# A fused residual kernel whose attention stage receives its row maxima through SyncE instead of GpSimd, with the first two bodies' score products made twice

## The chip, the cores and the metric

The kernel runs on one core of one Trainium2 chip. Its time is the device time of one execution, in microseconds (us). The engines are TensorE (PE in the profile, PEld for its weight loads), VectorE (DVE), ScalarE (ACT), GpSimd (POOL) and SyncE (SP, which here only issues DMAs). The kernel before takes 488.98 us, the median of 3 runs (486.17 to 490.18).

## What is computed

The input `x` is [16, 128, 128]: 16 batches of 128 positions with 128 features. Four residual steps follow each other:

```
x = x + L0(x)   # reflected second differences along both axes and a growth term, per-batch factors
x = x + L1(x)   # 8 gated experts and a shared one: (silu(x @ Wg) * (x @ Wu)) @ Wd, weighted per batch
x = x + L2(x)   # low-rank product with the batch's language, and the language's embedding
x = x + L3(x)   # attention, 16 heads of 8 features
```

The attention is the step that matters here:

```
query = seq2 + b_self
key = jnp.concatenate([seq1 + b_prev, seq2 + b_self], 1)
...
score_prev = jnp.einsum('bhqd,bhkd->bhqk', q, k[:, :, :l1]) * SCALE
score_self = (q * k[:, :, l1:]).sum(-1, keepdims=True) * SCALE
mask = jnp.arange(l1)[None, :] < seq_len1[:, None]
...
weights = jax.nn.softmax(jnp.concatenate([score_prev, score_self], -1), axis=-1)
attn = jnp.einsum('bhqk,bhkd->bhqd', weights[..., :-1], v[:, :, :l1])
attn = attn + weights[..., -1:] * v[:, :, l1:]
```

Each query attends to the 128 masked positions of one sequence and to one score of its own; the softmax subtracts each row's maximum over both.

## The kernel before, in words

**Stages.** The 16 batches are taken as four tiles of 4 (TB). The first 379 us are the experts: for each tile, 36 slots (`SLOTS`) of gate, up and down products, each product as three matmuls of rounded parts (`three`, L516 to L518). The last 110 us are the attention, one `body` for each batch b from 0 to 15; bodies 2 to 13 run in a loop of four bodies. The low-rank step and the keys and values of the last tile (`LAST_AUX`: lora_a, lora_b, key, value, x_natural) are spread over bodies 0 and 1.

**Data of a batch.** Queries and keys are kept in HBM as rows (`q_rows`, `k_rows`). SP loads them for a pair p of batches (2p and 2p + 1): `load_first(p)` fills `k_blocks` and `q_plain` (4 DMAs of 96 KB, one of 16 KB, one of 384 KB), `load_second(p)` fills `q_blocks` and `k_plain` (4 of 96 KB, one of 384 KB). There are two buffers of each.

**Two score products.** `scores(b, i)` (into `s_ps`, L585) gives scores with the queries on the partitions; VectorE reduces each to row maxima (`max_group`, L1151) and merges them (`merge_max`, L1159). It is made two bodies ahead: body b makes the scores of b + 2. GpSimd negates and splits the maxima (`split_max`, L1361 to L1366), TensorE turns them (`turn_max`, L592), ScalarE copies them out as `max_rows` (`copy_max`, L868), and two DMAs of 8 KB (`place_max`, L1351) put them as two more rows into `q_blocks`. `scores_t(b, i)` (into `st_ps`, L684) then gives the transposed scores with the maximum already subtracted, ScalarE takes the exponential (`exp_scores`, L915), and `weigh` (L694) multiplies with the values. `scores_t(b, 0)` is the instruction that waits for the two DMAs (`max_placed`). After that come `take_pv` (ACT), `turn_pv` (PE, L703), `normalise` (DVE, L1214 to L1220), `turn_attn` (PE, L709), `copy_attn` (ACT, L935) and `project` (PE, L713), each one or two batches late.

**What sets the order.** Every engine runs its own written list in order, with semaphore waits. In body b TensorE turns the maxima of b + 2 at the end. GpSimd in body b does `split_max(b + 2)`, `weigh_self(b)`, `place_max(b + 2)`. So `max_rows` go through GpSimd's own DMA queue (q0 in the profile), while SP's DMAs are on q1. SP's list after the first four loads is `step(p)` for each pair: `load_first(p + 2)` once the scores of batches up to 2p + 1 are written, `load_second(p + 1)` once the transposed scores up to 2p - 1 are written, then `store_out(p - 3)`. Ahead of `step(2)` stand `later_stores(NT - 1)`: six DMAs of 128 KB that put the last tile's key rows into HBM. The last tile's steps and `turn_max` use one and the same PSUM bank (`aux_ps` and `max_ps` are the same eighth of PSUM), `out_ps` is the bank that the experts' `acc_ps` leaves.

## Time and profile before

| | |
|---|---|
| median of 3 runs | 488.98 us (486.17 to 490.18) |
| profiled execution | 490.55 us; its span, first to last instruction, 488.7 us |
| busy over the span | PE 441.0 us, DVE 341.5, ACT 273.2, POOL 210.9 |
| mean granted TensorE clock | 0.952 of full speed |
| DMA | 30.68 MB, of which q1 (SP and ACT) 29.99 MB, q0 (GpSimd) 0.26 MB |

Times of rows are us from the start of the span. A row of the timeline has start, duration, engine, line, operation with output and inputs, shape and count; in square brackets stands how long the engine was idle before it and what ended that. A matmul's duration is longer than its share of the engine, since matmuls overlap: the engine's share is the distance between starts. "issue" after an arrow says that the profile names no releaser. The start of a batch in the attention is read here as the start of its first `scores_t`, the first L684 row of a body.

### The profile page before, as it was taken

How to read it: one execution, taken by the hardware profiler on the slowest of the kernel's cores; microseconds unless marked ns; L12 is line 12 of the kernel's file. 1: busy time of each engine (PE TensorE's matmuls, PEld its weight loads, DVE VectorE, ACT ScalarE, POOL GpSimd, SP SyncE). 2: the span in 40 equal slices, each digit the busy share in tenths (PEclk: the TensorE clock that was granted, in tenths of full speed). 3: DMA queues.
4: the chain of work that ended last, by engine and by line, in shares of the span. 5: the costliest groups of instructions: out<-in, count | busy, mean ns of one | idle time of the engine just before them, and what ended most of it. 6: DMA issues, size and time to landing. Idle time of an engine off the chain costs nothing.

```text
span 488.7 us, 7752 instructions
## 1 busy us (share of the span) xinstructions
PE 441.0 (90%) x2278; PEld 330.3 (68%) x2278; DVE 341.5 (70%) x594; ACT 273.2 (56%) x544; POOL 210.9 (43%) x261
## 2 busy tenths in 40 slices
PE   5789699779999998999999999999999778888894
PEld 2668578567678787867878686787787354545552
DVE  5787567597777779677768967776796666565552
ACT  2647556546465555545565554556556546565573
POOL 4667666883223434222244323228557333243340
PEclk9889979989999999999999999999999898797798
DMA  5423322300002020000201000022025256555320
GB/s 155 128 72 108 124 66 83 110 23 22 2 0 87 1 67 0 21 0 0 83 3 53 11 0 1 0 65 67 0 67 145 56 158 171 134 128 139 78 58 23
DMA packets 28147, 30.68 MB, mean 63 GB/s; under 512 B 4084, under 2 KB 22616, under 8 KB 28120
## 3 DMA queue, kind: packets, MB, share of 16 engines
q1 hardware_dynamic: 26664, 29.99, 21.8%
q0 software_dynamic: 1024, 0.26, 0.3%
q8 instruction: 13, 0.21, 0.2%
q10 hardware_dynamic: 432, 0.10, 0.1%
q14 instruction: 14, 0.11, 0.1%
HBM read 22.73 MB, written 7.35 MB: 62 GB/s over the span
## 4 chain that ended last, share of the span: by engine, by line
PE 63%; DVE 13%; DMA 8%; ACT 6%; issue 5%; POOL 4%; DVEq 0%; ACTq 0%; SPq 0%; POOLq 0%
PE acc_ps L516 6%; PE g_ps L516 5%; PE acc_ps L518 5%; PE g_ps L518 5%; PE acc_ps L517 5%; PE g_ps L517 5%; DVE act_lo L1086 5%; PE u_ps L516 5%; PE u_ps L518 4%; PE u_ps L517 4%; DMA w_raw<-in_L_cond_Wu 4%; DVE act_p L1082 3%; DMA q_blocks<-max_rows 3%; PE pv_ps L694 2%; PE s_ps L585 2%
## 5 line engine op out<-in xcount | busy, mean ns | idle before, releaser
L815 ACT ACTIVATE act_p<-g_ps 128x512 f32<-128x512 f32 x144 | 86.0, 597 | 135.2 <-PE g_ps L518 120.5
L1082 DVE TENSOR_TENSOR act_p<-act_p,u_ps 128x512 f32<-128x512 f32 x144 | 98.6, 685 | 71.5 <-PE u_ps L518 44.5
L1086 DVE TENSOR_TENSOR act_lo<-act_p,act_hi 128x512 fp32r<-128x512 f32 x144 | 121.1, 841 | 0.2 <-ACT act_hi L820 0.2
L1296 POOL TENSOR_TENSOR xg_lo<-xg,xg_hi 128x512 fp32r<-128x512 f32 x35 | 50.5, 1442 | 147.1 <-ACT xg_hi L825 147.1
L820 ACT ACTIVATE act_hi<-act_p 128x512 fp32r<-128x512 f32 x144 | 89.8, 624 | 3.8 <-DVE act_p L1082 3.5
L516 PE MATMUL acc_ps<-act_hi,w_split 128*128 128x512 f32 x144 | 62.0, 430 | 16.8 <-DVE act_lo L1086 16.7
L516 PE MATMUL g_ps<-x_hi,w_split 128*128 128x512 f32 (+1 forms) x144 | 57.8, 402 | 1.4 <-DVE x_lo L1112 1.4
L518 PE MATMUL acc_ps<-act_hi,w_split 128*128 128x512 f32 x144 | 57.2, 397 | 0.0
L516 PE MATMUL u_ps<-xg_hi,w_split 128*128 128x512 f32 x144 | 57.0, 396 | 0.1
L518 PE MATMUL g_ps<-x_hi,w_split 128*128 128x512 f32 (+1 forms) x144 | 56.9, 395 | 0.0
L517 PE MATMUL g_ps<-x_lo,w_split 128*128 128x512 f32 (+1 forms) x144 | 56.9, 395 | 0.0
L517 PE MATMUL acc_ps<-act_lo,w_split 128*128 128x512 f32 x144 | 56.9, 395 | 0.0
L517 PE MATMUL u_ps<-xg_lo,w_split 128*128 128x512 f32 x144 | 56.5, 392 | 0.0
L518 PE MATMUL u_ps<-xg_hi,w_split 128*128 128x512 f32 x144 | 56.4, 392 | 0.0
L1285 POOL TENSOR_TENSOR w_split<-w_raw,w_split 128x512 fp32r<-128x512 f32 x27 | 40.1, 1487 | 27.2 <-ACT w_split L786 27.2
L516 PEld LDWEIGHTS acc_ps<-act_hi,w_split 128*128 128x128 f32 x144 | 27.3, 189 | 34.5 <-DVE act_lo L1086 24.0
L1151 DVE TENSOR_REDUCE max_key<-s_ps 128x4 f32<-128x512 f32 x56 | 36.4, 685 | 14.2 <-PE s_ps L585 13.4
L1292 POOL TENSOR_TENSOR xg<-x,gates 128x512 f32 (+1 forms) x35 | 40.9, 1169 | 5.8 <-ACT x L795 3.6
L684 PE MATMUL st_ps<-q_blocks,k_plain 98*128 98x512 f32 x64 | 31.1, 490 | 8.9 <-DMA q_blocks<-max_rows 5.8
L516 PEld LDWEIGHTS g_ps<-x_hi,w_split 128*128 128x128 f32 x144 | 27.5, 191 | 7.3 <-DVE x_lo L1112 1.7
L516 PEld LDWEIGHTS u_ps<-xg_hi,w_split 128*128 128x128 f32 x144 | 27.5, 191 | 6.6 <-issue 0.5
L518 PEld LDWEIGHTS g_ps<-x_hi,w_split 128*128 128x128 f32 x144 | 27.5, 191 | 6.1
(161 smaller groups left out, 718.2 us busy)
## 6 DMA issues: line engine op xcount, KB each, us to landing
k_blocks<-k_rows SPq DMA_DIRECT2D x32, 96.0 KB
q_plain<-q_rows SPq DMA_DIRECT2D x8, 384.0 KB
q_blocks<-q_rows SPq DMA_DIRECT2D x32, 96.0 KB
k_plain<-k_rows SPq DMA_DIRECT2D x8, 384.0 KB
w_raw<-in_L_cond_Wg SPq DMA_DIRECT2D x8, 256.0 KB, 2.7
w_raw<-in_L_cond_Wu SPq DMA_DIRECT2D x8, 256.0 KB, 2.9
w_raw<-in_L_cond_Wd SPq DMA_DIRECT2D x8, 256.0 KB, 2.8
q_rows<-rows_hi SPq DMA_DIRECT2D x16, 128.0 KB
```

The lines of the kernel that those rows point to most:

```text
L516: mm(dst, w_h, x_h, start=start, stop=False)
L517: mm(dst, w_h, x_l, start=False, stop=False)
L518: return mm(dst, w_l, x_h, start=False, stop=stop)
L684: mm(st_ps[i % 2][:], k_plain[n // 2 % 2][0:ROWS + 2, i, half(n)], q_blocks[n // 2 % 2][0:ROWS + 2, :, i, half(n)], start=True, stop=True) ...
L815: activation(act_p[k % 3][:], g_ps[k % 3][:], ACT.Silu).then_inc(silu_done, 1)
L820: activation(act_hi[k % 3][:], act_p[k % 3][:], ACT.Identity).then_inc(act_hi_done, 1)
L1082: tt(act_p[k % 3][:], act_p[k % 3][:], u_ps[k % 3][:], ALU.mult).then_inc(prod_done, 1)
L1086: tt(act_lo[k % 3][:], act_p[k % 3][:], act_hi[k % 3][:].bitcast(F32), ALU.subtract).then_inc(act_lo_done, 1)
L1151: nc.vector.tensor_reduce(max_key[n % 2][:, i], (s_ps[i % 2] if bank is None else bank)[:].rearrange("p (j s) -> p j s", j=GJ), AX_X, ALU. ...
L1285: tt(w_lo[:, w // 3, w % 3], w_raw[w % 3][:], w_hi[:, w // 3, w % 3].bitcast(F32), ALU.subtract)\
L1292: tt(xg[:], x1[:, t], over_s(gates[:, e, bass.ds(t * TB, TB)]), ALU.mult).then_inc(xg_made, 1)
L1296: tt(xg_lo[e % 3][:], xg[:].rearrange("p b s -> p (b s)"), xg_hi[e % 3][:].bitcast(F32), ALU.subtract)\
```

## The change

Four things are moved or rewritten, and one is added.

1. SP issues the two DMAs of `max_rows`. Its list becomes: `step(0)`; then for each batch b a wait for `max_copied` and `place_max(b)`; after each odd b from 3 on `step(b // 2)`; after batch 3 also the last tile's six row stores.
2. `turn_max(b + 1)` stands in body b behind the first score product, where `turn_max(b + 2)` stood at the end of it; ScalarE's `copy_max` and `exp_self` move likewise. `turn_attn(b - 2)` and its copy move forward to the middle of the body, `project` to before the last `scores_t`.
3. The last tile's steps use `out_ps`, so the waits for `max_copied` ahead of them and for `aux_drained` ahead of `turn_max` go; one wait is put ahead of the first `turn_attn`.
4. The own weight and the weighted own value lie in one buffer `own_w`, so that `normalise` has three instructions where it had four; GpSimd does `weigh_self(b)` first.
5. In bodies 0 and 1 every score product, of both kinds, is issued twice with the same operands and output (`FIRST_RUNS`).

```diff
+FIRST_RUNS = 2
+LAST_STORES = 3
...
-        self_exp = [sb2(f"self_exp{n}", [128, H]) for n in range(4)]
+        own_w = [sb2(f"own_w{n}", [128, H, DH + 1]) for n in range(4)]
...
+        def later_ps(t):
+
+            return out_ps if isinstance(t, int) and t == NT - 1 else aux_ps
...
+            def place_max(b):
+
+                for c in range(2):
+                    sp.dma_start(q_blocks[b // 2 % 2][ROWS + c:ROWS + c + 1, :, :, b % 2 * S:(b % 2 + 1) * S]
+                                 .rearrange("p j i s -> p (j i) s").bitcast(F32),
+                                 max_rows[b % 2][c * H:(c + 1) * H]).then_inc(max_placed[b % 2], 16)
+
...
-            for p in range(NP + 3):
-                if p == 2:
+            step(0)
+            for b in range(B):
+                sp.wait_ge(max_copied, b + 1)
+                place_max(b)
+                if b % 2 and b > 1:
+                    p = b // 2
+                    if p == NP - 4:
+                        sp.wait_ge(rows_stored, ROW_STORES * 2 * NT)
+                    step(p)
+                if b == LAST_STORES:
                     later_stores(NT - 1)
-                if p == NP - 4:
-                    sp.wait_ge(rows_stored, ROW_STORES * 2 * NT)
+            for p in range(NP, NP + 3):
                 step(p)
             sp.wait_ge(out_stored, 16 * NP)
...
-                kind = LATER_AUX[m]
+                kind, ps = LATER_AUX[m], later_ps(t)
-                    last = mm(aux_ps[0:64, :], lora_a_t[:], x1[:, t].rearrange("p b s -> p (b s)"), start=True, stop=True)
+                    last = mm(ps[0:64, :], lora_a_t[:], x1[:, t].rearrange("p b s -> p (b s)"), start=True, stop=True)
...
-                mm((s_ps[i % 2] if bank is None else bank)[:], q_plain[n // 2 % 2][0:ROWS + 1, i, half(n)],
-                   k_blocks[n // 2 % 2][0:ROWS + 1, :, i, half(n)], start=True, stop=True).then_inc(s_written, 1)
+                for _ in range(FIRST_RUNS if isinstance(b, int) and bank is None else 1):
+                    last = mm((s_ps[i % 2] if bank is None else bank)[:], q_plain[n // 2 % 2][0:ROWS + 1, i, half(n)],
+                              k_blocks[n // 2 % 2][0:ROWS + 1, :, i, half(n)], start=True, stop=True)
+                last.then_inc(s_written, 1)
...
-                mm(st_ps[i % 2][:], k_plain[n // 2 % 2][0:ROWS + 2, i, half(n)],
-                   q_blocks[n // 2 % 2][0:ROWS + 2, :, i, half(n)], start=True, stop=True).then_inc(st_written, 1)
+                for _ in range(FIRST_RUNS if isinstance(b, int) and b < 2 else 1):
+                    last = mm(st_ps[i % 2][:], k_plain[n // 2 % 2][0:ROWS + 2, i, half(n)],
+                              q_blocks[n // 2 % 2][0:ROWS + 2, :, i, half(n)], start=True, stop=True)
+                last.then_inc(st_written, 1)
...
             def last_tile_step(b, i):
                 if isinstance(b, int) and (b, i) in LAST_AUX:
-                    pe.wait_ge(max_copied, b + 2)
                     later_step(LAST_AUX[b, i], NT - 1)
-            def body(b, n, s_next=True):
-
-                for i in range(2):
-                    if s_next:
-                        scores(b + 2, n + 2, i)
-                    scores_t(b, n, i)
+            def body(b, n, s_next=True, turn_next=True):
+
+                if s_next:
+                    scores(b + 2, n + 2, 0)
+                if n >= 1 and turn_next:
+                    turn_max(b + 1, n + 1)
+                scores_t(b, n, 0)
+                if s_next:
+                    scores(b + 2, n + 2, 1)
+                scores_t(b, n, 1)
                 last_tile_step(b, 1)
                 if n >= 1:
                     weigh(b - 1, n - 1, 0)
                     weigh(b - 1, n - 1, 1)
+                if n == 2:
+                    pe.wait_ge(aux_drained, LAST_STEP + 4)
+                if n >= 2:
+                    turn_attn(b - 2, n - 2)
                 if s_next:
                     scores(b + 2, n + 2, 2)
                     scores(b + 2, n + 2, 3)
                     weigh(b - 1, n - 1, 2)
                     weigh(b - 1, n - 1, 3)
                 if n >= 2:
-                    turn_attn(b - 2, n - 2)
+                    project(b - 2, n - 2)
                 scores_t(b, n, 3)
                 last_tile_step(b, 3)
-                if n >= 2:
-                    project(b - 2, n - 2)
                 if n >= 1:
                     turn_pv(b - 1, n - 1)
-                if isinstance(b, int) and b < 2:
-                    pe.wait_ge(aux_drained, LAST_STEP + (1 if b == 0 else 4))
-                if s_next:
-                    turn_max(b + 2, n + 2)
...
-                body(b, b % TB, s_next=False)
+                body(b, b % TB, s_next=False, turn_next=b + 1 < B)
...
-                activation(self_exp[n % 4][:], self_arg[n % 2][:], ACT.Exp).then_inc(self_exp_done, 1)
+                activation(own_w[n % 4][:, :, DH], self_arg[n % 2][:], ACT.Exp).then_inc(self_exp_done, 1)
...
-            def body(b, n, s_next=True):
+            def body(b, n, turn_next=True):
                 exp_scores(b, n, 0)
+                if n >= 1 and turn_next:
+                    copy_max(b + 1, n + 1)
+                    exp_self(b + 1, n + 1)
                 exp_scores(b, n, 1)
                 last_tile_step(b, 1)
                 if n == 0:
                     act.wait_ge(v_ones_set, 2)
                 place_values(b, n)
+                if n >= 2:
+                    copy_attn(b - 2, n - 2)
                 exp_scores(b, n, 2)
                 last_tile_step(b, 2)
                 if n >= 1:
                     take_pv(b - 1, n - 1)
-                if n >= 2:
-                    copy_attn(b - 2, n - 2)
                 exp_scores(b, n, 3)
-                if s_next:
-                    copy_max(b + 2, n + 2)
-                    exp_self(b + 2, n + 2)
...
-                dve.wait_ge(self_exp_done, b + 1)
-                tt(denom[n % 2][:], pv[:, :, DH], self_exp[n % 4][:], ALU.add).then_inc(norm_step, 1)
                 dve.wait_ge(self_weighted, b + 1)
-                tt(numer[n % 2][:], pv[:, :, 0:DH], v_self_w[n % 2][:], ALU.add).then_inc(norm_step, 1)
-                dve.wait_ge(norm_step, b * 3 + 2)
-                nc.vector.reciprocal(rdenom[n % 2][:], denom[n % 2][:]).then_inc(norm_step, 1)
-                dve.wait_ge(norm_step, b * 3 + 3)
-                tt(attn[n % 2][:], numer[n % 2][:], rdenom[n % 2][:].unsqueeze(2).to_broadcast([128, H, DH]),
+                tt(numer[n % 2][:], pv[:, :, 0:DH + 1], own_w[n % 4][:], ALU.add).then_inc(norm_step, 1)
+                dve.wait_ge(norm_step, b * 2 + 1)
+                nc.vector.reciprocal(rdenom[n % 2][:], numer[n % 2][:, :, DH]).then_inc(norm_step, 1)
+                dve.wait_ge(norm_step, b * 2 + 2)
+                tt(attn[n % 2][:], numer[n % 2][:, :, 0:DH], rdenom[n % 2][:].unsqueeze(2).to_broadcast([128, H, DH]),
                    ALU.mult).then_inc(attn_done, 1)
...
-            def weigh_self(b, n, place_next):
+            def weigh_self(b, n):
                 wait(pool, attn_done, b - 1)
                 pool.wait_ge(self_exp_done, b + 1)
-                if place_next:
-                    pool.wait_ge(max_copied, b + 3)
                 own = own_values[:].rearrange("p t (b x) -> p (t b) x", b=TB)[:, b].rearrange("p (h r) -> p h r", r=DH)
-                tt(v_self_w[n % 2][:], own, self_exp[n % 4][:].unsqueeze(2).to_broadcast([128, H, DH]),
-                   ALU.mult).then_inc(self_weighted, 1)
+                w = own_w[n % 4]
+                tt(w[:, :, 0:DH], own, w[:, :, DH:DH + 1].to_broadcast([128, H, DH]), ALU.mult).then_inc(self_weighted, 1)
             def body(b, n, s_next=True):
+                weigh_self(b, n)
                 if s_next:
                     split_max(b + 2, n + 2)
-                weigh_self(b, n, s_next)
-                if s_next:
-                    place_max(b + 2, n + 2)
                     pick_mask(b + 2, n + 2)
             for b in range(2):
-                pool.wait_ge(max_copied, b + 1)
-                place_max(b, b)
                 pick_mask(b, b)
```

SP's list in the attention, from the third pair's first loads on; `max_rows` are the maxima, `rows_hi` and `rows_lo` the last tile's keys. Before:

```order
L453 DMA k_blocks<-k_rows 24x1024 x4
L464 DMA k_blocks<-mask_row 1x16x256
L457 DMA q_plain<-q_rows 96x1024
L453 DMA k_blocks<-k_rows 24x1024 x4
L464 DMA k_blocks<-mask_row 1x16x256
L457 DMA q_plain<-q_rows 96x1024
L453 DMA q_blocks<-q_rows 24x1024 x4
L457 DMA k_plain<-k_rows 96x1024
L390 DMA k_rows<-rows_hi 4x32x256 x4
L390 DMA k_rows<-rows_lo 4x32x256 x2
L453 DMA k_blocks<-k_rows 24x1024 x4
```

And now:

```order
L457 DMA k_blocks<-k_rows 24x1024 x4
L468 DMA k_blocks<-mask_row 1x16x256
L461 DMA q_plain<-q_rows 96x1024
L487 DMA q_blocks<-max_rows 1x16x128 x8
L457 DMA k_blocks<-k_rows 24x1024 x4
L468 DMA k_blocks<-mask_row 1x16x256
L461 DMA q_plain<-q_rows 96x1024
L457 DMA q_blocks<-q_rows 24x1024 x4
L461 DMA k_plain<-k_rows 96x1024
L394 DMA k_rows<-rows_hi 4x32x256 x4
L394 DMA k_rows<-rows_lo 4x32x256 x2
L487 DMA q_blocks<-max_rows 1x16x128 x4
```

The eight rows of maxima DMAs are batches 0 to 3; those of batches 4 and 5 stand behind the 11 loads and the 6 stores. From there on four such DMAs (an even and an odd batch) stand between one pair's loads and the next.

TensorE's list at the start of the attention, bodies 0 and 1. Before, with `lora_a_t` and `lora_b_t` the last tile's low-rank step and L592 the turning of the maxima:

```order
L585 MATMUL s_ps<-k_blocks,q_plain 128x512
L684 MATMUL st_ps<-q_blocks,k_plain 128x512
L585 MATMUL s_ps<-k_blocks,q_plain 128x512
L684 MATMUL st_ps<-q_blocks,k_plain 128x512
L562 MATMUL aux_ps<-x,lora_a_t 64x512
L585 MATMUL s_ps<-k_blocks,q_plain 128x512 x2
L684 MATMUL st_ps<-q_blocks,k_plain 128x512
L564 MATMUL aux_ps<-dif_a,lora_b_t 128x512
L684 MATMUL st_ps<-q_blocks,k_plain 128x512
L592 MATMUL max_ps<-squares,neg_max 32x128
L585 MATMUL s_ps<-k_blocks,q_plain 128x512
L684 MATMUL st_ps<-q_blocks,k_plain 128x512
```

And now:

```order
L604 MATMUL s_ps0<-k_blocks1,q_plain1 128x512 x2
L705 MATMUL st_ps0<-q_blocks0,k_plain0 128x512 x2
L604 MATMUL s_ps1<-k_blocks1,q_plain1 128x512 x2
L705 MATMUL st_ps1<-q_blocks0,k_plain0 128x512 x2
L580 MATMUL out_ps<-x1,lora_a_t 64x512
L604 MATMUL s_ps0<-k_blocks1,q_plain1 128x512 x2
L604 MATMUL s_ps1<-k_blocks1,q_plain1 128x512 x2
L705 MATMUL st_ps0<-q_blocks0,k_plain0 128x512 x2
L582 MATMUL out_ps<-dif_a,lora_b_t 128x512
L705 MATMUL st_ps1<-q_blocks0,k_plain0 128x512 x2
L604 MATMUL s_ps0<-k_blocks1,q_plain1 128x512 x2
L612 MATMUL max_ps<-squares,neg_max0 32x128
```

Four more products stand ahead of the first low-rank product, and the first turning (L612, batch 2) comes behind the first score product of body 1 instead of ahead of it.

## Rows read from the trace of the kernel before

**Rows 1.** Timeline of TensorE: the first `scores_t` of batches 3 to 14, in order.

```profile
402.43 0.50 PE L684 MATMUL st_ps<-q_blocks,k_plain 98*128 98x512 f32 x1 [1.66 <-DMA q_blocks<-max_rows]
...
408.22 0.40 PE L684 MATMUL st_ps<-q_blocks,k_plain 98*128 98x512 f32 x1
...
416.55 0.47 PE L684 MATMUL st_ps<-q_blocks,k_plain 98*128 98x512 f32 x1 [2.98 <-issue]
...
423.08 0.63 PE L684 MATMUL st_ps<-q_blocks,k_plain 98*128 98x512 f32 x1
...
429.58 0.49 PE L684 MATMUL st_ps<-q_blocks,k_plain 98*128 98x512 f32 x1 [0.76 <-DMA q_blocks<-max_rows]
...
434.44 0.46 PE L684 MATMUL st_ps<-q_blocks,k_plain 98*128 98x512 f32 x1
...
441.19 0.47 PE L684 MATMUL st_ps<-q_blocks,k_plain 98*128 98x512 f32 x1 [1.75 <-DMA q_blocks<-max_rows]
...
448.28 0.57 PE L684 MATMUL st_ps<-q_blocks,k_plain 98*128 98x512 f32 x1
...
455.09 0.50 PE L684 MATMUL st_ps<-q_blocks,k_plain 98*128 98x512 f32 x1 [1.60 <-DMA q_blocks<-max_rows]
...
462.40 0.39 PE L684 MATMUL st_ps<-q_blocks,k_plain 98*128 98x512 f32 x1
...
472.27 0.70 PE L684 MATMUL st_ps<-q_blocks,k_plain 98*128 98x512 f32 x2
```

**Rows 2.** Timeline of SP: the first loads of each pair, and the last tile's stores.

```profile
391.22 1.52 SPq L453 DMA_DIRECT2D k_blocks<-k_rows  x4
...
395.98 3.26 SPq L390 DMA_DIRECT2D k_rows<-rows_hi  x4
399.29 2.84 SPq L390 DMA_DIRECT2D k_rows<-rows_lo  x2
404.82 1.92 SPq L453 DMA_DIRECT2D k_blocks<-k_rows  x4
...
419.23 1.52 SPq L453 DMA_DIRECT2D k_blocks<-k_rows  x4
...
431.85 1.53 SPq L453 DMA_DIRECT2D k_blocks<-k_rows  x4
...
444.45 1.91 SPq L453 DMA_DIRECT2D k_blocks<-k_rows  x4
```

**Rows 3.** Timeline of GpSimd: maxima of batches 3 and 5; then the tile's landing times.

```profile
396.18 1.03 POOL L1351 DMA_DIRECT2D q_blocks<-max_rows  x2
...
409.18 1.03 POOL L1351 DMA_DIRECT2D q_blocks<-max_rows  x2
...
DMA to landing us min/median/max: 1.7/2.7/6.7
```

**Rows 4.** Windows: length, busy PE, PEld, DVE, ACT, POOL, granted clock, DMA share, GB/s.

```profile
386.50:395.00 8.50, 7.93 (x62) 5.67 (x63) 4.86 (x10) 4.48 (x10) 2.44 (x9) 0.80 0.18 57
...
403.00:404.00 1.00, 1.00 (x19) 0.49 (x18) 0.69 (x1) 1.00 (x2) 0.12 (x1) 1.00 0.27 97
...
405.30:405.60 0.30, 0.30 (x12) 0.27 (x12) 0.30 (x1) 0.30 (x1) 0.00 (x0) 0.50 0.26 89
...
418.00:419.00 1.00, 1.00 (x6) 0.81 (x3) 0.19 (x1) 0.61 (x3) 0.00 (x0) 0.50 0.00 0
...
428.80:429.00 0.20, 0.02 (x1) 0.00 (x0) 0.17 (x2) 0.20 (x2) 0.00 (x0) 1.00 0.00 0
```

**Rows 5.** Timeline of TensorE, bodies 0 and 1: low-rank products and turnings.

```profile
382.22 1.10 PE L564 MATMUL aux_ps<-dif_a,lora_b_t 68*128 68x512 f32 x2 [0.41 <-DVE dif_a L1058]
...
386.46 0.27 PE L592 MATMUL max_ps<-squares,neg_max 128*32 128x128 f32 x1 [2.92 <-issue]
...
395.00 0.28 PE L592 MATMUL max_ps<-squares,neg_max 128*32 128x128 f32 x1 [0.57 <-DVE x L1070]
```

**Rows 6.** Timeline of ScalarE and TensorE, a body at full clock: the late copies.

```profile
437.98 0.27 ACT L935 ACTIVATE attn_t<-out_ps 128x128 f32<-128x128 f32 x1
...
438.31 0.49 PE L713 MATMUL out_ps<-w_raw,attn_t 128*128 128x128 f32 x2 [0.17 <-ACT attn_t L935]
```

More of the change, by code:

```diff
@@ L210, in build @@
         pv_own = [sb2(f"pv_own{n}", [128, HALVES, S]) for n in range(2)]
-        v_self_w = [sb2(f"v_self_w{n}", [128, H, DH]) for n in range(2)]
-        denom = [sb2(f"denom{n}", [128, H]) for n in range(2)]
         rdenom = [sb2(f"rdenom{n}", [128, H]) for n in range(2)]
-        numer = [sb2(f"numer{n}", [128, H, DH]) for n in range(2)]
+        numer = [sb2(f"numer{n}", [128, H, DH + 1]) for n in range(2)]
         attn = [sb2(f"attn{n}", [128, H, DH]) for n in range(2)]
@@ L570, in later_step @@
                         tok = slice(b * S, (b + 1) * S)
-                        last = three(aux_ps[:, tok], in_hi[:, tok], in_lo[:, tok], w_qkv_h[:, 2], w_qkv_l[:, 2])
+                        last = three(ps[:, tok], in_hi[:, tok], in_lo[:, tok], w_qkv_h[:, 2], w_qkv_l[:, 2])
                 else:
                     for b in range(TB):
-                        last = turn(aux_ps[:, b * S:(b + 1) * S], x3_t[:, b], ident)
+                        last = turn(ps[:, b * S:(b + 1) * S], x3_t[:, b], ident)
                 last.then_inc(aux_written, 1)
@@ L809, in later_step @@
                     act.wait_ge(rows_stored, (2 * NT - 1) * ROW_STORES if isinstance(t, int) and t == NT - 1 else t * (2 * ROW_STORES) + 2 * ROW_STORES)
-                    activation(rows_hi[:], aux_ps[:], ACT.Identity, bias=cols[:, 1:2]).then_inc(aux_rounded, 1)
+                    activation(rows_hi[:], later_ps(t)[:], ACT.Identity, bias=cols[:, 1:2]).then_inc(aux_rounded, 1)
             def silu(t, k):
@@ L966, in _ @@
             for b in range(B - 2, B):
-                body(b, b % TB, s_next=False)
+                body(b, b % TB, turn_next=b + 1 < B)
             take_pv(B - 1, B - 1)
@@ L1345, in _ @@
                         nc.gpsimd.memset(tile[:].bitcast(F32), constant).then_inc(blocks_filled, 1)
-            def place_max(b, n):
-                for c in range(2):
-                    pool.dma_start(q_blocks[n // 2 % 2][ROWS + c:ROWS + c + 1, :, :, n % 2 * S:(n % 2 + 1) * S]
-                                   .rearrange("p j i s -> p (j i) s").bitcast(F32),
-                                   max_rows[n % 2][c * H:(c + 1) * H]).then_inc(max_placed[n % 2], 16)
             def split_max(b, n):
```

16 lines of the change are left out of this document (8 added, 8 removed).

## The prediction

> **What bounds the kernel now.** I read the stretches first, then TensorE's order of work in the attention, then what it waits for. The experts (to 379 us) are untouched. The change lives in the last 110 us, and there I read where each batch starts [rows 1]. Batches 12 and 13 show what two bodies need when nothing holds them: 472.27 - 462.40 = 9.9 us, 4.9 us each. From batch 4 to batch 12 eight bodies take 462.40 - 408.22 = 54.2 us, 6.8 each. The 15 us between are two things. First, the odd batches 3, 5, 7, 9 and 11 wait 1.66, 2.98, 0.76, 1.75 and 1.60 us, 8.8 in all, in front of their first `scores_t` [rows 1]; the 2.98 has no releaser named, but the same instruction waits for the same DMAs. Second, behind each of these waits but the shortest TensorE's granted clock falls: in the window 418 to 419 us it is 0.50, 1.2 instead of 2.4 GHz [rows 4]. The body pairs behind such a wait show the price: 448.28 - 441.19 = 7.1 and 462.40 - 455.09 = 7.3 us for one body, so 2.3 us over 4.9 [rows 1]. After 0.76 us there is no such price (434.44 - 429.58 = 4.9).
>
> Why the odd ones? SP's loads of a pair start at 404.82, 419.23, 431.85 and 444.45 us [rows 2]; call such a moment L. The maxima of the odd batch are issued behind it (batch 5: 409.18 [rows 3]) and TensorE goes on at 416.55, 429.58, 441.19, 455.09 [rows 1], that is L + 11.7, 10.4, 9.3 and 10.6, on average **L + 10.5**. An 8 KB transfer in a free machine lands in 1.7 to 2.7 us [rows 3]; here it lands when the pair's 1.57 MB are through. In the window 428.80 to 429.00 nothing moves any more [rows 4], and TensorE resumes 0.8 us after 428.8. So it is the loads, and not GpSimd's two issues of 1.03 us together [rows 3], that make these waits.
>
> **The change part by part.** Times below are of the profiled execution (490.55 us, span 488.7), which lies 1.57 above the median of 488.98.
>
> *Doubled products, body 0.* A product costs TensorE 0.70 - 0.47 = 0.23 us at full clock (two in 0.70, one in 0.47 [rows 1]). Four more ahead of the first low-rank product are 0.92 us; the second low-rank product waits for VectorE, which waits for the first [rows 5], and splitting, merging and the first turning (386.46) hang behind. Three more in between push it another 0.1 or 0.2. So the first turning comes 1.1 us later. The 2.92 us that TensorE idles before it [rows 5] cover the two other copies, of `scores_t(0, 3)` and of body 1's first score product.
>
> *Doubled products, body 1.* Behind the turning remain seven copies. Three come while the clock is low after that idle time (it shrinks to 2.2 us, and waits of 1.60 and more were all followed by the low clock): 3 x 0.46 = 1.4; four at full clock, 0.9. Against that the first score product has moved ahead of the turning (0.3), and the wait of 0.57 us for `x` [rows 5] is gone, since the last tile has a bank of its own. One score product now precedes the next turning (0.3). Batch 3's turning: 395.00 + 1.1 + 2.3 - 0.9 + 0.3 = **397.8 us**.
>
> *SP's place.* The copy starts 0.3 us after the turning and takes 0.3; two issues on SP are not in this trace. The nearest rows are GpSimd's pair, 1.03 us [rows 3], and SP's loads, 0.38 each (four in 1.52 [rows 2]), 0.8 for two; I take 1.0. So L comes 1.65 us after the odd batch's turning: L = 399.45 for pair 3.
>
> *Batch 4.* SP's list has the loads and the six stores ahead of batch 4's maxima. Before, the same run of DMAs started at 391.22 and 395.98 and was issued by 402.13 [rows 2]. The stores move slowly: from 403 to 404 us the DMA engines are 0.27 busy at 97 GB/s, and at 405.3 to 405.6 still 0.26 [rows 4], so the stores are through at about 405.6, L + 14.4 (6 x 128 KB at 97 GB/s are 8.1 us). The Trainium skill (DMA: Bandwidth & Descriptors, "Why a DMA increments its semaphore by 16 and not by 1") says that such a DMA runs on as many engines, up to 16, as divide the slowest dimension of both sides, here four; the share of 0.27 agrees. With 0.8 us of landing batch 4 starts at 399.45 + 14.4 + 0.8 = **414.7** where it was 408.22. Its own need is 397.9 + 2 x 4.7 = 407.3, so TensorE stands 7 us. This stall is new: GpSimd's queue delivered batch 3's maxima, issued at 396.18, by 402.43 [rows 1, 3], while the stores were still under way. Bounds: issued at L + 10.9 and landed 2.7 later it is L + 14.6, 0.6 earlier; stores that begin only when the loads are through end at L + 9.7 + 8.1 = L + 17.8, 3.4 later. I take what the same run of DMAs showed.
>
> *The body itself.* ScalarE's copy of `attn` (0.27) and the projection behind it [rows 6] leave the chain from the last exponentials to the end of a body, 0.5 us; `normalise` loses one small instruction. But the turning now stands ahead of `scores_t`, and GpSimd's three small operations ahead of it give back 0.1. So a body needs 4.5 us instead of 4.9 (bounds 4.4 and 4.9), and 6.8 at the low clock.
>
> *From batch 6 on.* One body at the low clock and one not: batch 6 at 414.7 + 6.8 + 4.5 = 426.0 (before 423.08). Batch 7's turning is then 0.15 before this, L = 425.85 + 1.65 = 427.5. Now the even batch is the one behind the loads: SP needs 395.98 - 391.22 = 4.8 us to issue them [rows 2] before it can issue batch 8's maxima, which wait in the same queue. I take L + 10.5 again, 438.0; bounds 9.3 and 11.7 of the rows, and 12.6 if a place at the end of the queue costs a further landing. Own need 426.0 + 9.0 = 435.0. Batch 8 starts at 438.0, 3.0 us late, and the clock falls. But batch 9's turning stands ahead of that wait (434.85, L = 436.5), so the next loads are under way during the stall: batch 10's maxima are there at 447.0, before its need of 438.0 + 11.3 = 449.3 (before 448.28). Batch 10 does not wait. L = 449.15 + 1.65 = 450.8, batch 12 at 461.3 (need 458.3), the clock falls, batch 14 at 461.3 + 11.3 = **472.6** where it was 472.27.
>
> *The end.* Bodies 14 and 15 are ScalarE's; batch 15's maxima have 1.65 us and 1.7 to 2.7 of landing in a free queue against a body of about 3.7, a wait of 0.6 us at most. I count nothing. GpSimd, rid of the issues, is not waited for.
>
> Sum: +0.3 us, less the 0.1 that three `normalise` at the end save each: **no change**. 490.55 + 0 against 488.98 + 1.57: the median comes to **489.0 us**.
>
> The Trainium skill (same page, "Latency and other measured facts") gives the first byte of a DMA issued by SP as about 0.6 us and by GpSimd as about 1 us. As an estimate by that page, landings 0.4 us earlier at batches 4, 8 and 12 would make the sum 1.2 us less, 487.8; no row here shows a maxima transfer of SP.
>
> **Rivals.** *The small transfer gets through early (0.31).* If maxima behind the loads land at L + 8.6, batch 8 is late by 1.1 us, which lies between 0.76 (clock held) and 1.60 (clock lost). If the clock holds, batch 8 is at 436.1, 10 at 445.1, 12 at 455.2, 14 at 464.2: 8.4 us gained, 480.6. With no wait left at 8, 10 and 12, batch 14 comes at 426.0 + 36 = 462.0 and the time is 478.7. For it: the loads start earlier in the body, half the stall disappears in any case, and two bodies in nine us is a strong lever. Against it: all four rows lie at 9.3 or later. The point: L + 9.
>
> *In order behind everything (0.18, the slower one).* On SP's queue a small transfer waits for every byte ahead of it. At batch 4 that is L + 17.8 + 0.8, 3.4 us more, at batches 8 and 12 L + 12.6, 2 x 2.1. Alone they give 492.4 and 493.2, together 496.6. The kernel is slower than before as soon as either is later than I took it, and by over 1% with the stores' 3.4 us and landings from L + 11.3 on (3.4 + 2 x 0.75 = 4.9). For it: batch 3's maxima overtook the stores from the other queue. The Trainium skill (same page, "Queues, rings and completion order") has each DMA engine take turns between queues packet by packet, and work one queue's ring in order. By that rule the change gives the turns away; the trace agrees at batch 3 and shows little of it behind the loads.
>
> *The copies hold the clock (0.10).* If the copies keep TensorE at 2.4 GHz through body 1, three of them cost 0.7 less; and from 386.5 to 395 the granted clock is 0.80 on average [rows 4], so 8.5 x 0.4 = 3.4 us of body 1 are at half speed now and would be done in 1.7. All behind comes 2.4 us earlier: 486.6. Against it: 2.2 us of idle time remain.
>
> *Nothing waits as thought (0.04):* the doubled products lie wholly in idle time and the stalls stay where they are, 489 as well.
>
> **The numbers.** My own case has 0.37, at 489.0 (486 to 492: landings between L + 9.3 and 11.7 are 2 x 1.2 us to either side, batch 4's lower bound 0.6). A measurement of this kernel can tell about 1%, 4.9 us, from no change: faster is below 484.1, slower above 493.9. Faster: the first rival and 0.05 of the low ends, 0.36. Slower: 0.14 of the second rival and 0.05 of the high ends, 0.19. Same: 0.45. The range goes from 478.5, no waits, to 495.5, most of the second rival.
>
> **What the changed kernel's profile would show.** TensorE idle 7 us ahead of batch 4's first `scores_t`, at about 414.7, with the DMA share at 0.27 just before. Waits of 2 to 3 us at batches 8 and 12 and none at 5, 7, 9, 10 and 11. SP's maxima rows of even batches right behind a pair's loads. Clock 0.50 behind batches 4, 8, 12. Batch 3's turning at 397.8. I am wrong if batch 4 starts before 411 (the stores don't hold it), if batch 8 starts at its need, or if every even batch waits 4 us.

## The result, and the profile after

The changed kernel takes **507.04 us** (median of 4 runs, 504.39 to 509.93) beside 489.58 for the kernel before; the ratio is 1.0372 [1.0297, 1.0448]. It is slower; the forecast was 489.0, no change, with a range from 478.5 to 495.5. The profiled execution took 504.39 us, its span is 502.6. Ratios here leave disturbed runs out, so they can differ a little from the quotient of the medians beside them.

The experts end at 377.08 us instead of 378.82, so the attention itself went from 109.9 to 125.5 us, 15.6 more. TensorE's timeline, first `scores_t` of batches 0, 2, 3, 4, 6, 8, 10, 12 and 14, to be laid beside [rows 1] (L705 is what L684 was):

```profile
382.51 1.19 PE L705 MATMUL st_ps<-q_blocks,k_plain 98*128 98x512 f32 x2 [4.80 <-DMA q_blocks<-max_rows]
...
401.50 0.50 PE L705 MATMUL st_ps<-q_blocks,k_plain 98*128 98x512 f32 x1
...
406.56 0.49 PE L705 MATMUL st_ps<-q_blocks,k_plain 98*128 98x512 f32 x1
...
422.50 0.79 PE L705 MATMUL st_ps<-q_blocks,k_plain 98*128 98x512 f32 x1 [10.61 <-DMA q_blocks<-max_rows]
...
435.78 0.50 PE L705 MATMUL st_ps<-q_blocks,k_plain 98*128 98x512 f32 x1 [2.39 <-DMA q_blocks<-max_rows]
...
449.02 0.50 PE L705 MATMUL st_ps<-q_blocks,k_plain 98*128 98x512 f32 x1 [2.70 <-DMA q_blocks<-max_rows]
...
462.83 0.49 PE L705 MATMUL st_ps<-q_blocks,k_plain 98*128 98x512 f32 x1 [3.01 <-DMA q_blocks<-max_rows]
...
476.13 0.50 PE L705 MATMUL st_ps<-q_blocks,k_plain 98*128 98x512 f32 x1 [2.88 <-DMA q_blocks<-max_rows]
...
487.77 0.71 PE L705 MATMUL st_ps<-q_blocks,k_plain 98*128 98x512 f32 x2
```

The odd batches no longer wait; of the even ones batches 0, 4, 6, 8, 10 and 12 do: 26.4 us in six waits, where it was 8.8 in five. Counted from the attention's start, batch 4 is at 45.4 us instead of 29.4, batch 14 at 110.7 instead of 93.4. So 16.0 us are lost by batch 4. From there to batch 12 a pair takes 13.4 us instead of 13.55, from batch 12 to 14 it takes 11.6 instead of 9.9, and 1.6 us come back behind batch 14. SP's timeline, as [rows 2], shows both places:

```profile
371.56 1.52 SPq L457 DMA_DIRECT2D q_blocks<-q_rows  x4
...
373.51 1.61 SPq L457 DMA_DIRECT2D k_blocks<-k_rows  x4
...
375.69 0.58 SPq L461 DMA_DIRECT2D q_plain<-q_rows  x1
376.32 27.71 SPq L487 DMA_DIRECT2D q_blocks<-max_rows  x8
404.07 1.77 SPq L457 DMA_DIRECT2D k_blocks<-k_rows  x4
...
409.35 2.86 SPq L394 DMA_DIRECT2D k_rows<-rows_hi  x4
412.25 3.20 SPq L394 DMA_DIRECT2D k_rows<-rows_lo  x2
415.49 9.83 SPq L487 DMA_DIRECT2D q_blocks<-max_rows  x4
425.37 1.76 SPq L457 DMA_DIRECT2D k_blocks<-k_rows  x4
```

*Start.* ScalarE had copied the maxima of batches 0 and 1 by 368.4 and 372.6 us (its two L891 rows), but in SP's list they stand behind pair 1's second loads (0.79 MB, held until 371.56 by the wait for `blocks_filled`) and behind `step(0)` (0.80 MB). They are issued at 376.32 and batch 0 waits 4.80 us, until 10.95 us after 371.56. *Batch 4.* L = 404.07, and TensorE goes on at 422.50, L + 18.4. The windows of the stall (columns as in [rows 4]):

```profile
411.60:413.00 1.40, 0.28 (x2) 0.00 (x0) 0.69 (x1) 0.00 (x0) 0.43 (x2) 0.83 0.78 205
413.00:421.00 8.00, 0.00 (x0) 0.00 (x0) 0.00 (x0) 0.00 (x0) 0.00 (x0) 0.50 0.29 99
421.00:422.50 1.50, 0.01 (x1) 0.01 (x1) 0.00 (x0) 0.00 (x0) 0.00 (x0) 0.50 0.10 34
```

For eight microseconds the DMA engines move 99 GB/s and no compute engine runs: the six stores take up the queue when the loads are through, and the maxima come behind them. *The later pairs.* ScalarE's timeline at batch 6:

```profile
436.32 0.69 ACT L938 ACTIVATE probs_t<-st_ps,mask_col 128x512 f32<-128x512 f32 x1 [3.30 <-PE st_ps L705]
436.91 0.25 ACT L891 ACTIVATE max_rows<-max_ps 32x128 f32<-32x128 f32 x1
```

TensorE turned batch 7's maxima at 433.11, but the copy (L891) stands in ScalarE's list behind the exponential of the very `scores_t` that is waiting. So L is 438.36, 5.25 us after the turning, and batch 8 starts at L + 10.7 = 449.02.

### The profile page after: what moved, and what is told of

Same layout as the page of the kernel before. It is cut to its first block, busy times and chain, and to the rows that moved or that the text cites. A ratio compares the mean times of both kernels' runs of the same rounds, so it can differ in the third digit from the quotient of the medians.

```text
span 502.6 us, 7748 instructions
## 1 busy us (share of the span) xinstructions
PE 442.7 (88%) x2294; PEld 331.6 (66%) x2294; DVE 335.7 (67%) x578; ACT 272.2 (54%) x544; POOL 193.4 (38%) x229
## 4 chain that ended last, share of the span: by engine, by line
PE 56%; DVE 12%; DMA 11%; SPq 7%; ACT 5%; issue 4%; POOL 4%; DVEq 0%; ACTq 0%; POOLq 0%
DMA q_blocks<-max_rows 6%; PE acc_ps L534 5%; PE g_ps L534 5%; PE g_ps L536 5%; PE g_ps L535 5%; DVE act_lo L1109 4%; PE acc_ps L536 4%; PE acc_ps L535 4%; PE u_ps L534 4%; PE u_ps L536 4%; PE u_ps L535 4%; DMA w_raw<-in_L_cond_Wu 3%; DVE act_p L1105 3%; SPq L457 3%; PE st_ps L705 3%
## 5 line engine op out<-in xcount | busy, mean ns | idle before, releaser
L1109 DVE TENSOR_TENSOR act_lo<-act_p,act_hi 128x512 fp32r<-128x512 f32 x144 | 119.3, 829 | 0.2 <-ACT act_hi L843 0.2
L705 PE MATMUL st_ps<-q_blocks,k_plain 98*128 98x512 f32 x72 | 33.6, 490 | 26.5 <-DMA q_blocks<-max_rows 26.4
L938 ACT ACTIVATE probs_t<-st_ps,mask_col 128x512 f32<-128x512 f32 x32 | 21.8, 681 | 45.8 <-PE st_ps L705 45.8
L705 PEld LDWEIGHTS st_ps<-q_blocks,k_plain 98*128 98x128 f32 x72 | 15.1, 215 | 31.8 <-DMA q_blocks<-max_rows 17.0
L1375 POOL TENSOR_TENSOR neg_max<-max_all,minus_one 128x16 fp32r<-128x16 f32 x14 | 3.1, 221 | 78.5 <-DVE max_all L1182 78.5
## 6 DMA issues: line engine op xcount, KB each, us to landing
q_plain<-q_rows SPq DMA_DIRECT2D x8, 384.0 KB
k_plain<-k_rows SPq DMA_DIRECT2D x8, 384.0 KB
```

The source lines that it names most:

```text
L705: last = mm(st_ps[i % 2][:], k_plain[n // 2 % 2][0:ROWS + 2, i, half(n)], q_blocks[n // 2 % 2][0:ROWS + 2, :, i, half(n)], start=True, sto ...
L1109: tt(act_lo[k % 3][:], act_p[k % 3][:], act_hi[k % 3][:].bitcast(F32), ALU.subtract).then_inc(act_lo_done, 1)
```

## The experiments

The four of the first group ran on one chip beside a kernel before of 489.3 us.

**Once instead of twice.**

```
-FIRST_RUNS = 2
+FIRST_RUNS = 1
```

> The changed kernel with every score product made once (only the doubling is undone). Theory A (the loss sits in SP's list and in the waits for maxima; the copies are a small part): the copies of body 0 stand behind batch 0's late maxima at the low clock (some 0.43 us each), those of body 1 at full clock (0.23), and 2.2 us of idle time ahead of the first turning hide a part; so 2 to 4 us less, about 504 us against 507, the 4.8 us wait at batch 0 and the 10.6 us wait at batch 4 unchanged. Theory B (the copies are what costs): back to the time of the kernel before, 489. Theory C (the copies hold the clock): 1 to 3 us more, with a low granted clock through body 1.

Measured 507.34 us, ratio 1.0386 [1.0271, 1.0501]. The waits are as theory A has them, 4.46 us at batch 0 and 10.61 at batch 4; the 2 to 4 us that it expected back are not there, though the interval, 5.6 us to either side, could hide them. The trace says more. TensorE's turning of batch 3's maxima and its start of batch 4:

```profile
401.99 0.28 PE L612 MATMUL max_ps<-squares,neg_max 128*32 128x128 f32 x1
...
424.14 0.79 PE L705 MATMUL st_ps<-q_blocks,k_plain 98*128 98x512 f32 x1 [10.61 <-DMA q_blocks<-max_rows]
```

The attention began at 379.54 here. Counted from that, the turning is at 22.5 us instead of 24.3 (401.33 after 377.08), batch 4 at 44.6 instead of 45.4, the end at 125.3 instead of 125.5. The doubling costs 1.8 us at first, and in these two executions almost nothing of it reaches the end.

**Stores two batches later.**

```
-LAST_STORES = 3
+LAST_STORES = 5
```

> The changed kernel with the last tile's six row stores behind batch 5's step in SP's list instead of batch 3's. Theory A (SP's queue is worked in order, so whatever maxima stand next behind the stores wait for them): batch 4 waits some 3 us instead of 10.6 (start at L + 10.6, L the first load of pair 3), but batch 6 now starts at L + 18.4 of the next loads, so the stall moves and the total stays within 2 us of 507. Theory B (only batch 4's place was unlucky, two bodies later there is slack for the stores): 7 to 9 us less, 498 to 500, and batch 6 waits no more than 3 us.

Measured 505.99, ratio 1.0366 [1.0281, 1.045]. TensorE's waits, batches 4, 6 and 8:

```profile
417.15 0.79 PE L705 MATMUL st_ps<-q_blocks,k_plain 98*128 98x512 f32 x1 [3.13 <-DMA q_blocks<-max_rows]
...
438.49 0.79 PE L705 MATMUL st_ps<-q_blocks,k_plain 98*128 98x512 f32 x1 [10.08 <-DMA q_blocks<-max_rows]
...
452.31 0.79 PE L705 MATMUL st_ps<-q_blocks,k_plain 98*128 98x512 f32 x1 [2.01 <-DMA q_blocks<-max_rows]
```

The stall went with the stores. With L = 405.97 and 420.02 from SP's rows, batch 4 comes at L + 11.2 without them and batch 6 at L + 18.5 with them: the stores are worth 7.3 us in front of whatever rows follow. This is theory A, in its waits and in its total.

**First maxima early.**

```
+            for b in range(2):
+                sp.wait_ge(max_copied, b + 1)
+                place_max(b)
             step(0)
```

> The changed kernel with the maxima DMAs of batches 0 and 1 ahead of step(0)'s loads in SP's list instead of behind them. Theory A (batch 0 waited 4.8 us for its 8 KB because they stood behind 0.8 MB of loads, and the low clock followed): batch 0 starts without a wait, the clock stays at 1.0 through body 0, the rest comes 5 to 8 us earlier: 499 to 502 us. Theory B (the time is given back at batch 4, whose wait for the stores sets the rest whatever comes before): batch 4 starts at the same time and the total moves by less than 2 us.

Measured 499.65, ratio 1.0229 [1.0147, 1.0311]; 7.4 us less than the changed kernel, by medians. Batch 0's wait is 0.91 us, the granted clock of its body is 1.00 (378.5 to 384.0 us), and batch 3's turning (396.02) is 5.2 us earlier, counted from the attention's start. Batch 4's wait is still there:

```profile
378.48 0.70 PE L709 MATMUL st_ps<-q_blocks,k_plain 98*128 98x512 f32 x2 [0.91 <-DMA q_blocks<-max_rows]
...
417.86 0.80 PE L709 MATMUL st_ps<-q_blocks,k_plain 98*128 98x512 f32 x1 [10.50 <-DMA q_blocks<-max_rows]
```

**Copy first on ScalarE.**

```
             def body(b, n, turn_next=True):
-                exp_scores(b, n, 0)
                 if n >= 1 and turn_next:
                     copy_max(b + 1, n + 1)
                     exp_self(b + 1, n + 1)
+                exp_scores(b, n, 0)
```

> The changed kernel with ScalarE's copy of batch b + 1's maxima ahead of body b's first exponential instead of behind it. Theory A (the even batches wait because the copy of the odd batch's maxima, SP's issue behind it and so the next pair's loads all stand behind the exponential that waits for the stalled scores): a pair's loads start at the turning + 1.7 us instead of at the even batch's start + 2.6; the wait at batches 6 and 10 goes or falls under 1 us, that at 8 and 12 stays at 2 to 3; pair period 11.5 instead of 13.3 us, total 5 to 8 us less, 499 to 502. Theory B (the even batches are bound by the transfer of the loads itself): the same 13.3 us per pair and the total within 2 us of 507.

Measured 498.87, ratio 1.0209 [1.0118, 1.0299]. The waits at batches 6 and 10 are gone, those at 8 and 12 stay (batch 6 stands at 435.83 with none):

```profile
423.46 0.80 PE L705 MATMUL st_ps<-q_blocks,k_plain 98*128 98x512 f32 x1 [11.28 <-DMA q_blocks<-max_rows]
...
448.95 0.79 PE L705 MATMUL st_ps<-q_blocks,k_plain 98*128 98x512 f32 x1 [3.54 <-DMA q_blocks<-max_rows]
...
473.12 0.80 PE L705 MATMUL st_ps<-q_blocks,k_plain 98*128 98x512 f32 x1 [2.82 <-DMA q_blocks<-max_rows]
```

This is the alternation that the prediction had described; it needed the copy ahead of the exponential. From batch 4 to batch 12 it takes 49.7 us, where the changed kernel takes 53.6 and the prediction had 46.6.

The next four ran beside a kernel before of 488.93 us. **GpSimd's queue** (abridged; `place_next` holds from body 1 to the last but one, and the issues of batches 0 and 1 move too).

```
-                place_max(b)                      # SP's list
+                if place_next:                    # GpSimd's body b
+                    pool.wait_ge(max_copied, b + 2)
+                if s_next:
+                    pick_mask(b + 2, n + 2)
+                if place_next:
+                    place_max(b + 1, n + 1)
                 weigh_self(b, n)
```

> The changed kernel with one thing taken back: GpSimd issues the max rows again on its own queue (batch b+1's in body b, as soon as ScalarE has copied them), and SyncE's list holds the loads, stores and outputs alone. The turning stays where the change put it, one body ahead, and the first two bodies are still doubled. Theory A (the time is lost by standing in SyncE's list behind a pair's loads and the last tile's stores): the long waits at batches 0 and 4 (4.80 and 10.61 us) go, a landing is 2 to 7 us after its issue, the even batches wait 0 to 2 us: 487 to 493 us. Rival B (the loss is that the maxima are turned one body ahead instead of two, on whichever queue): waits of 2 to 3 us stay at the even batches and some come at the odd ones: 496 to 504 us.

Ratio 1.0109 [1.0005, 1.0212] (median 498.99, 491.98 to 500.02). By ratio the queue alone is worth 2.6% (by medians 8 us, 1.6%). The waits at batches 0 and 4 are gone, as theory A has it, but there are six others, 1.5 to 3.8 us and 18.4 in all, at the odd batches 3 to 13, as rival B has it; the median lies in rival B's range. Two things can make up what stays: these waits, which were 8.8 us in the kernel before, and the doubling, which costs as much alone (the last experiment). They are not told apart.

**The kernel before, with SyncE issuing.**

```
+                if p < NP:
+                    place_max(2 * p)
+                if p == 0:
+                    place_max(1)
                 step(p)
+                if 0 < p < NP:
+                    place_max(2 * p + 1)
```

> The kernel before with one thing changed: SyncE issues the max rows, in this order: batches 0 and 1, then for each later pair its even batch, the loads, its odd batch. The turning stays at the end of body b for batch b+2, and nothing is doubled. Theory A2 (the queue costs only because the turning is late; with a body to spare the 10.5 us behind the loads are covered): waits of 0 to 2 us at the odd batches: 487 to 493 us. Rival B2 (rows behind a pair's loads are always late on this queue): a wait of 3 us or more in each pair: 500 to 506 us.

Ratio 1.0113 [1.0033, 1.0192] (median 496.12), between the two theories. Waits are 0.7 to 3.7 us in six (batches 0, 4, 5, 7, 9 and 11), longest at batch 9:

```profile
448.92 0.77 PE L698 MATMUL st_ps<-q_blocks,k_plain 98*128 98x512 f32 x1 [3.73 <-DMA q_blocks<-max_rows]
```

Its loads start at 437.57, so this is L + 11.3. A body to spare does not quite cover a landing behind the loads.

**Both repairs.**

The edits of the third and fourth experiment together.

> The changed kernel with both repairs that were run alone: SyncE sends the max rows of batches 0 and 1 before the pair's loads (alone 499.65 us), and ScalarE copies batch b+1's turned maxima ahead of body b's first exponential (alone 498.87 us). The stores stay behind batch 3's rows. Theory A (two separate losses, at the start and at the even batches 6 to 12): they add, 490 to 493 us, with a wait of 10 to 11 us left at batch 4. Rival C (both gave back the same thing, the clock or the start): 496 to 500 us.

Ratio 1.0173 [1.0092, 1.0254], median 492.42. The median is in the range of theory A; the ratio, 2.0% below the changed kernel's, is less than the sum of the two (1.4 and 1.6%) and agrees with it only within the intervals. Applied to the first group's 489.3 us, it gives 497.8, in rival C's range, so whether the two losses add is left open by the times. The trace has the waits that theory A expected: 0.59 at batch 0, 10.72 at 4, 3.52 at 8, 3.82 at 12, none at 6 and 10.

**GpSimd's queue, copy first, each product once.**

The edits of the first, fourth and fifth experiment together.

> As e5_gpsimd_queue, with ScalarE copying batch b+1's maxima ahead of the first exponential, and each product made once. Of the changed kernel only the turning one body ahead, the denominator's column and the order of the bodies are left. Theory A: no wait for a max row over 1 us, 483 to 489 us, so at or a little below the kernel before. Rival B (turned too late on any queue): 492 to 500 us.

Measured 486.81, ratio 0.9988 [0.9945, 1.0032]: the kernel before again, though by another way. The time is in theory A's range, but not for its reason: it had no wait over 1 us, and six waits of 1.4 to 3.8 us are left, at the odd batches 3 to 13. The copy and the doubling were changed together here, so neither has a price of its own. Batch 7, GpSimd's issue of its rows and TensorE's start:

```profile
421.87 1.03 POOL L1363 DMA_DIRECT2D q_blocks<-max_rows  x2 [0.29 <-issue]
```

```profile
428.19 0.49 PE L696 MATMUL st_ps<-q_blocks,k_plain 98*128 98x512 f32 x1 [2.00 <-DMA q_blocks<-max_rows]
```

SP's loads of the pair began at 417.21: L + 11.0. From another queue too, rows issued 4.7 us into the loads land when the loads are through.

The next three ran beside a kernel before of 487.41 us. **SyncE's list reordered** (against the seventh experiment, abridged).

```
             for b in range(B):
+                if b % 2 and b > 1:
+                    step(b // 2)
                 if b > 1:
                     sp.wait_ge(max_copied, b + 1)
                     place_max(b)
-                if b % 2 and b > 1:
-                    step(b // 2)
```

> As e7_two_repairs_on_sync (ratio 1.0173), with SyncE's list reordered: of each later pair the even batch's max rows come ahead of the loads and the odd batch's behind them (e7: both ahead of the loads, so that the next pair's even batch is behind them). SyncE alone issues, the turning stays one body ahead, the first two bodies are doubled. Theory A (the waits at the even batches are the ring's: rows issued behind 1.57 MB of loads): the even batches wait 0 to 1.5 us, the odd ones have a body to spare and wait 0 to 2; batch 4 waits under 4 us: 484 to 490 us, ratio 0.99 to 1.00. Rival B (the turning one body ahead is too late on this queue in any order): waits of 3 us move to the odd batches, 492 us or more, ratio 1.01 or more.

Ratio 1.0109 [1.0054, 1.0165] (median 496.58): rival B. The waits moved to the odd batches, 3.89 and 3.64 us at 7 and 9:

```profile
432.28 0.79 PE L709 MATMUL st_ps<-q_blocks,k_plain 98*128 98x512 f32 x1 [3.89 <-DMA q_blocks<-max_rows]
...
447.45 0.47 PE L709 MATMUL st_ps<-q_blocks,k_plain 98*128 98x512 f32 x1 [3.64 <-issue]
```

With the loads at 421.11 and 436.29 both are L + 11.2. In the three orders tried on SP's list (this one, the seventh and the sixth experiment) some batch was always behind the loads.

**Loads behind the rows** (the eighth experiment and one line).

```
+                    sp.wait_ge(max_placed[0], 32 * (p + 1))
                     step(p)
```

> As e8_gpsimd_copy_once (486.81 us), and SyncE issues a pair's loads only when the even batch's max rows, which GpSimd sent in the same body, have landed. Theory A (what is left of the waits, 1.4 to 3.8 us at batches 2 to 12 in e8's profile, is the loads sharing the 16 DMA engines with the rows on the other queue): they fall under 1 us each, 478 to 483 us. Rival D (the rows take 2 to 3 us by themselves, or the loads come too late now and the next pair waits for them): 485 to 490 us.

(The batches 2 to 12 of this expectation are the odd ones, 3 to 13.) Measured **477.29 us, ratio 0.9707 [0.9627, 0.9787]**, a little below theory A's range and faster than both kernels, by one wait on SP. SP's loads and GpSimd's rows around batch 6 and 7, then TensorE's start of batches 6 and 8:

```profile
416.15 1.53 SPq L457 DMA_DIRECT2D k_blocks<-k_rows  x4
...
426.96 1.53 SPq L457 DMA_DIRECT2D k_blocks<-k_rows  x4
```

```profile
411.83 1.03 POOL L1364 DMA_DIRECT2D q_blocks<-max_rows  x2 [0.29 <-issue]
...
416.58 1.03 POOL L1364 DMA_DIRECT2D q_blocks<-max_rows  x2 [0.29 <-issue]
```

```profile
416.27 0.50 PE L697 MATMUL st_ps<-q_blocks,k_plain 98*128 98x512 f32 x1 [0.71 <-DMA q_blocks<-max_rows]
...
421.08 0.49 PE L697 MATMUL st_ps<-q_blocks,k_plain 98*128 98x512 f32 x1
...
426.95 0.50 PE L697 MATMUL st_ps<-q_blocks,k_plain 98*128 98x512 f32 x1 [1.07 <-DMA q_blocks<-max_rows]
```

A pair takes 10.7 us. Batch 6's rows land before the loads begin; batch 7's go out 0.4 us behind the loads' first issue, not 4.7, and are there by 421.08, when TensorE comes for them without a wait. The waits sum to 5.5 us in five, the longest 1.46 (theory A had each under 1), where the kernel without the gate had 13.2 in six, and the clock is granted in full from 415 to 427 us:

```profile
417.00:419.00 2.00, 2.00 (x33) 1.23 (x36) 1.35 (x3) 1.72 (x6) 1.06 (x3) 1.00 0.71 191
```

The five waits are now at batches 3, 6, 8, 10 and 12, and those of the even batches have the old cause: batch 8's rows, issued at 422.17 behind all the loads of 416.15, have landed when the gate lets the next loads go at 426.96, 10.8 us after those. The first loads of the pairs come at 405.99, 416.15, 426.96 and 437.27, so one pair's loads follow the other's at once, and what is left of a pair's 10.7 us is about the time of its loads.

**Two ahead again, on GpSimd.**

The eighth experiment with `turn_max`, `copy_max` and `place_max` of b + 2 at the places of the kernel before.

> As e8_gpsimd_copy_once, with the turning, its copy and its rows put back two bodies ahead (the order of the kernel before); what is left of the change is the denominator's column, the place of the attention's turning and projection in a body, and the last tile's products in another bank. Theory A (e8's lead over the kernel before is in those parts, and a turning two bodies ahead waits no more than in the kernel before): 480 to 486 us. Rival E (with the copy first, one body ahead is as good, and the later turning behind the body's end holds TensorE): 486 to 491 us.

Measured 484.0, ratio 0.9902 [0.9849, 0.9954]: theory A. Its waits sum to 8.8 us, as in the kernel before. So the rest of the change (the denominator's column, the body's order, the last tile's bank) is a gain of 1%, 0.3 us a body, where the prediction had 0.4. Turning two ahead is about 1% better than one ahead without the gate, though the two intervals just touch.

**The doubling alone** (kernel before 488.38 us; shown for the transposed products, the other kind likewise).

```
+                for _ in range(FIRST_RUNS if isinstance(b, int) and b < 2 else 1):
                     last = mm(st_ps[i % 2][:], ...)
```

> The kernel before with the other half of the change alone: in the first two bodies each of the 8 score products and 8 transposed ones is made twice (16 more products of 0.23 to 0.63 us); queue, turning and bodies are as before. Theory A (the doubling costs nothing, as e1_once showed beside the wait at batch 0: bodies 0 and 1 wait for GpSimd's, VectorE's and ScalarE's chain at least as long): within 1.5 us of the kernel before, ratio 0.997 to 1.003. Rival F (where nothing waits at batch 0, the 16 products lengthen the first two bodies: before them 7.9 and 8.7 us, in e5_gpsimd_queue with the doubling 8.2 and 10.5 us): 2 to 4 us slower, ratio 1.004 to 1.008. Rival G (the copies hold the clock up): the clock of the first two bodies over 0.9 and 1 to 3 us faster.

Measured 491.85, ratio 1.0102 [1.0048, 1.0157]: rival F, above its upper end of 1.008, which the interval includes. The turning behind body 1 comes 19.9 us after the attention's start instead of 16.2:

```profile
386.62 0.37 PE L595 MATMUL max_ps<-squares,neg_max 128*32 128x128 f32 x1 [2.69 <-issue]
...
397.85 0.28 PE L595 MATMUL max_ps<-squares,neg_max 128*32 128x128 f32 x1 [0.57 <-DVE x L1075]
```

and the granted clock of that body (387.0 to 395.6 us) is 0.70 where the same window of the kernel before has 0.80. The copies did not hold the clock. The two profiled executions differ less at the end than at this turning, 110.6 us of attention against 109.9, so the 5 us rest on the times alone; what the trace shows is 3.7 us at batch 3's turning.

## Why the prediction was wrong, step by step

- **The start: missed.** The prediction took the doubled products as the only thing new in bodies 0 and 1 and put batch 3's turning at 397.8. It is at 401.33, in an attention that began 1.7 us earlier, so 5.3 late. The order that failed it is in the diff: `step(0)` ahead of `place_max(0)`. Taken out alone, it brings that turning 5.2 us forward and gives 7.4 us back.
- **"L comes 1.65 us after the odd batch's turning": the step that cost most.** It counted ScalarE's copy as following the turning at once and forgot that ScalarE's list is in order too. L comes 2.7 us after the turning where nothing waits (401.33 to 404.07) and 5.3 to 6.0 after it where the even batch does (433.11 to 438.36, 446.04 to 452.02). "Batch 10 does not wait" and the 6.2 us that the missing odd waits were to give back between batches 4 and 14 rested on it; measured, that stretch lost 1.2 us more. With the copy first, L comes 1.9 to 2.2 us after the turning at batches 7, 9 and 11, and batches 6 and 10 do not wait, as the prediction has it. From batch 4 to 12 this is worth 4.0 of the 7.0 us by which the changed kernel is over the forecast; the other 3.0 were not taken apart (landings and bodies were both somewhat longer than forecast).
- **Batch 4: right mechanism, too small.** L + 18.4 (18.5 in the second experiment, up to 19.5 in the fourth) instead of L + 15.2; the slower rival's L + 18.6, with stores that begin only when the loads are through, is what happened. The stall is 10.6 us, not 7. The Trainium skill (DMA: Bandwidth & Descriptors, "Queues, rings and completion order") has each DMA engine work one queue's ring in order; the traces agree, with maxima that come behind the stores wherever these are put, and the rival that stood on it deserved more than 0.18. The prediction's own reading, that the stores were through at 405.6 before, was wrong:

```profile
391.22:405.60 14.38, 11.81 (x118) 7.35 (x121) 9.70 (x23) 7.72 (x20) 4.83 (x16) 0.95 0.52 151
```

  These are 14.38 x 151 = 2.17 MB since L, of the 2.38 MB of a pair's loads and the six stores. By this count 0.2 MB of the stores were still to come, at 97 GB/s some 2 us (an estimate). The DMA share rises behind 405.6 (0.62 in 405.6 to 406.0) with the next pair's loads, issued from 404.82 on; the stores need not have ended for it.
- **The landing behind the loads: right.** 10.4, 10.7, 10.8 and 10.7 us behind L at batches 6 to 12, forecast 10.5; the other kernels with the maxima on SP's queue gave 10.3 to 12.2 (the longest in the first experiment, batch 10: 454.40 to 466.55).
- **The body of 4.5 us: right in direction, half the gain.** From turning to turning, where TensorE does not wait, it is 5.0 and 5.25 us in bodies 2 and 3 and 4.65, 4.7, 4.9 and 4.5 in those from body 5 on, against 4.9 before. **At the low clock** the prediction had 6.8; the bodies behind the waits take 5.6 to 6.3, the one of batch 4 at a mean granted clock of 0.69.
- **The doubling: sized about right, and small beside the rest.** The forecast had batch 3's turning 2.8 us later for it and for what moves with it; it is 3.7 later with the doubling alone, and 2.9 later, counted from the attention's start, in the changed kernel with the start's order repaired. In the time it costs 5 us (2 to 8) alone and nothing that the first experiment could see here, where batch 0 waits for its rows anyway.
- **The other parts, by ratio:** SP issuing costs 1.1% in the kernel before and 2.6% in the changed one, of which the start's order is 1.4%; the body's parts give 1% back. These overlap, so they are sizes and not a sum.

The loss of 15.6 us in the attention is then: 7.6 by batch 2, of which 4.8 is batch 0's wait, 8.4 more by batch 4, and in sum nothing (-0.4) behind it, where 6 us of gain had been forecast.

## What to carry to other kernels

Before a small transfer is moved to a queue that also carries bulk loads, write that queue's list down in order and ask for each small transfer how many bytes stand ahead of it; here a row landed 10.3 to 12.2 us after the first of a pair's loads, 1.57 MB, and 18.4 to 19.5 with six slow stores on top. Then look for the loop: if what starts the bulk loads waits, on any engine's in-order list, for the consumer of the small transfer, every period can pay the landing, as it did here. The cheapest repair found was to hold the bulk loads until the small transfer has landed. It was tried with the rows on GpSimd's queue only, and took the ratio from 0.9988 to 0.9707: the next loads went out as soon as the last were through, so holding them opened no gap between one pair's loads and the next.

## What was not expected of the hardware

- A second queue did not get small transfers past running loads: issued 4.7 us into a pair's loads from GpSimd they landed 6.3 us later, with the loads (L + 11.0), while those issued 0.4 us into them were there within 4.5. The Trainium skill (same page and section) says that an engine takes turns between queues packet by packet; the second case can be that, the first shows how little it may help. In the first case SP had issued ten of the pair's eleven loads, in the second at most four; no run changes this alone, so that it is the reason is not shown.
- The granted clock fell to 0.50 (1.2 GHz) in the wait of 4.8 us at batch 0 and stayed there while TensorE was fully busy again, 382.5 to 388.0 us:

```profile
382.50:388.00 5.50, 5.49 (x10) 2.76 (x11) 1.33 (x3) 1.67 (x4) 0.00 (x0) 0.50 0.00 0
```
